# Group 0 of a four-layer sequence kernel in another order, and the modulator product inside the first gate logit

## The reference

```
h1  = gelu(x3 @ Wn1.T + bn1)                    # line 846, ACT
mod = 0.5 + sigmoid(h1 @ Wn2.T + bn2)           # line 1284 on PE, 855 on ACT
wg  = sigmoid(concat(x3, ema(x3)) @ Wg.T + bg)  # gate logits on PE, scan 1729, tanh 868
tr  = ema(x3 * wg * mod[d], tau[d])  for d in 0, 1   # lines 1737 to 1750 on DVE
out = layernorm((gelu(x3 @ Wsoma.T) * sigmoid(blend(tr) @ Wtemp.T)) @ Wout.T)
```

## Time and profile before

| | us |
|---|---|
| median of 3 runs | 690.83 (690.83 to 690.85) |
| the profiled execution, own time | 691.58 |
| span of the profiled execution | 689.8 |
| PE busy in it | 652.3 |
| DVE busy in it | 551.5 |
| ACT busy in it | 370.0 |
| POOL busy in it | 176.1 |

### The profile page before, as it was taken

How to read it: one execution, slowest core, us unless ns; L and a number is a source line. 1 busy time by engine, 2 the same in 40 slices (tenths; PEclk the granted TensorE clock), 3 DMA queues, 4 the chain that set the end, 5 groups by cost and what they waited for, 6 DMA issues and landing times.

```text
span 689.8 us, 8219 instructions
## 1 busy us (share of the span) xinstructions
PE 652.3 (95%) x2848; PEld 491.8 (71%) x2848; DVE 551.5 (80%) x792; ACT 370.0 (54%) x759; POOL 176.1 (26%) x268
## 2 busy tenths in 40 slices
PE   3989989899899999999999999999999999999996
PEld 1545444477677878787878787888787878787875
DVE  2685877869997998799879987998799749974955
ACT  1143368666476357635764576357635743574244
POOL 5003412211065025411441154114411210121001
PEclk9999999999999999999999999999999999999999
DMA  6988999996048844562456335634463320031001
GB/s 205 329 304 287 269 248 313 335 342 163 0 56 156 152 64 100 119 95 54 101 133 104 60 94 116 96 62 98 111 97 61 50 74 0 1 56 68 1 0 61
DMA packets 51575, 86.83 MB, mean 126 GB/s; under 512 B 8256, under 2 KB 10304, under 8 KB 51406
## 3 DMA queue, kind: packets, MB, share of 16 engines
q0 software_dynamic: 16896, 33.56, 30.5%
q1 hardware_dynamic: 31134, 52.74, 21.3%
q10 hardware_dynamic: 3504, 0.01, 0.3%
HBM read 63.22 MB, written 22.04 MB: 124 GB/s over the span
## 4 chain that ended last, share of the span: by engine, by line
PE 60%; DVE 22%; ACT 7%; issue 6%; DMA 3%; SPq 1%; POOLq 0%; POOL 0%; ACTq 0%; DVEq 0%
PE bank L1177 16%; PE bank L1178 16%; PE bank L1179 16%; DVE tr L1750 5%; PE bank L1074 3%; DVE tr L1741 2%; ACT mod L855 2%; DVE wgb L1737 2%; DMA xts<-in_xT 2%; PE bank L1173 2%; DVE wgb L1729 2%; PE bank L1253 2%; DMA beside_scratch<-xts 1%; DVE tr L1758 1%; ACT wgb L868 1%
## 5 line engine op out<-in xcount | busy, mean ns | idle before, releaser
L1750 DVE TENSOR_TENSOR_SCAN tr<-alpha,carry,tr 128x512 f32<-128x512 f32 x48 | 58.9, 1267 | 0.0
L642 POOL TENSOR_TENSOR rs_a<-ss_a,consts 128x1 f32<-128x1 f32 x32 | 16.0, 499 | 143.3 <-ACT junk_f L822 143.0
L1177 PE MATMUL bank<-th,wg_l 128*128 128x512 f32 x128 | 51.9, 406 | 0.0
L1177 PE MATMUL bank<-xh,wg_l 128*128 128x512 f32 x128 | 51.9, 406 | 0.0
L1178 PE MATMUL bank<-xl,wg_h 128*128 128x512 f32 x128 | 50.5, 394 | 0.0
L1178 PE MATMUL bank<-tl,wg_h 128*128 128x512 f32 x128 | 50.5, 394 | 0.0
L1179 PE MATMUL bank<-xh,wg_h 128*128 128x512 f32 x128 | 50.2, 392 | 0.0
L1179 PE MATMUL bank<-th,wg_h 128*128 128x512 f32 x128 | 50.2, 392 | 0.0
L874 ACT ACTIVATE carry<-tr 128x2 f32<-128x2 f32 x32 | 6.6, 206 | 80.3 <-DVE tr L1750 80.3
L1737 DVE SCALAR_TENSOR_TENSOR wgb<-wgb,soma 128x512 f32<-128x512 f32 x32 | 22.0, 687 | 30.5 <-ACT wgb L868 30.5
L602 POOL TENSOR_TENSOR late_side_f<-x2b 128x510 f32<-128x510 f32 x24 | 28.3, 1177 | 56.8 <-DMA x2b<-x_scratch 26.1
(11 more groups left out here) (290 smaller groups left out, 2011.3 us busy)
## 6 DMA issues: line engine op xcount, KB each, us to landing
x2b<-beside_scratch POOLq DMA_DIRECT2D x12, 1024.0 KB, 9.1
xr<-rows_scratch POOLq DMA_DIRECT2D x10, 1024.0 KB, 10.2
xb<-in_x SPq DMA_DIRECT2D x8, 1024.0 KB, 14.6
result<-xr SPq DMA_DIRECT2D x7, 1024.0 KB, 4.3
beside_scratch<-xts SPq DMA_DIRECT2D x6, 1024.0 KB, 11.2
x2b<-rows_scratch POOLq DMA_DIRECT2D x6, 1024.0 KB, 10.9
x_scratch<-xb SPq DMA_DIRECT2D x5, 1024.0 KB, 13.0
x2b<-x_scratch SPq DMA_DIRECT2D x5, 1024.0 KB, 5.5
```

Source lines behind the costliest of these rows:

```text
L642: po.tensor_tensor(rs[:, c:c + 1], ss[:, c:c + 1], eps, ALU.add).then_inc(chain, 1)
L1177: pe.matmul(acc, wl, xh_, start=start, stop=False)
L1750: ve.tensor_tensor_scan(t[:, d], alpha[:, 1 + d:2 + d].broadcast_to([P, GN]), t[:, d], 0.0 if first else carry[:, k, 1 + d:2 + d], ALU.mul ...
```

## The change

In group 0, and at its border with the head:

- **PE**: the x3 transposes of group 0 come before the last three pooled products (tiles 13, 14, 15) instead of after them.
- **DVE**: `ln_apply(0, c)` are no longer alternated with x1 tiles; x1 of tiles 9 to 12 follow the fourth `ln_apply`; then the zeroed edge, `x3_lo(0)`, `late_by_local(2, 0)`, x1 of tiles 13 to 15, `weight2_low(1)`, and only then `late_stencil(2, 0)`.
- **ACT**: `x3_evict(0)` comes before `late_mix(2, 0)`; `weight_hi(0)` and the GELU follow at once; `late_mix(2, 1)` comes after the GELU; `scale_beside(6)` and `scale_beside(7)` move behind `late_mix(2, 2)` and `late_mix(2, 3)`, into the traces of group 0.
- **SP**: `store_beside(6)` comes after `store_x1(7)` and the load of the temporal weight.

In all eight groups, on PE: the modulator product (line 1284) stands between the two halves of gate logit 0 (after 12 of its 24 matmuls) instead of after all 24.

```diff
--- before.py
+++ after.py
@@ -501,11 +501,11 @@
                             sp.wait_ge(x1_done, NT + 1)
                             sp.dma_start(ws_st, chunks(wsoma)).then_inc(w2_in[0], 16)
                     store_x1(6)
-                    store_beside(6)
                     store_x1(7)
                     sp.wait_ge(x1_out[4], 16)
                     sp.wait_ge(x1_out[5], 16)
                     sp.dma_start(wt_st[:], chunks(wtemp)).then_inc(w2_in[1], 16)
+                    store_beside(6)
                     store_beside(7)
                     sp.wait_ge(x1_out[6], 16)
                     sp.wait_ge(x1_out[7], 16)
@@ -990,17 +990,16 @@
                     scale_beside(4)
                     scale_beside(5)
                     act.wait_ge(x1_out[3], 16)
+                    x3_evict(0)
                     late_mix(2, 0)
-                    x3_evict(0)
-                    late_mix(2, 1)
-                    scale_beside(6)
                     weight_hi(0, ws_h[:], ws_st)
-                    scale_beside(7)
                     for g in range(GROUPS):
                         adapted = g < LAST
                         late = g + 3 < GROUPS
                         n1_gelu(g)
-                        if 0 < g and g + 2 < GROUPS:
+                        if g == 0:
+                            late_mix(2, 1)
+                        elif g + 2 < GROUPS:
                             late_mix(g + 2, GT - 1)
                         mod_tanh(g)
                         keep_ctx(g, 0)
@@ -1008,12 +1007,14 @@
                         mod_affine(g)
                         if g == 0:
                             late_mix(2, 2)
+                            scale_beside(6)
                         keep_traces(g, 0)
                         keep_ctx(g, 1)
                         sigmoid_gate(g, 1)
                         trace_hi(g, 0)
                         if g == 0:
                             late_mix(2, 3)
+                            scale_beside(7)
                         keep_traces(g, 1)
                         keep_ctx(g, 2)
                         sigmoid_gate(g, 2)
@@ -1275,25 +1276,29 @@
                                 pe.wait_ge(o_w, GT * (g - 1) + k - 1)
                             elif k == 2:
                                 pe.wait_ge(x1_done, NT * B)
-                            gate_logits(g, k).then_inc(ctx_mm, 1)
+                            logits_now(g, k)
                             if k == 0:
-                                pe.wait_ge(x3T_hi, KE * g + 3)
-                                pe.wait_ge(n1_act, g + 1)
-                                if g == 0:
-                                    pe.wait_ge(wn2_set, 2)
-                                pe.matmul(bank[MOD][:], wn2_half[:], nar[:], start=True, stop=True)\
-                                  .then_inc(mod_mm, 1)
-
-                    def gate_logits(g, k):
-                        acc = bank[CTX[k]][:]
+                                modulators(g)
+                            logits_before(g, k).then_inc(ctx_mm, 1)
+
+                    def modulators(g):
+                        pe.wait_ge(x3T_hi, KE * g + 3)
+                        pe.wait_ge(n1_act, g + 1)
+                        if g == 0:
+                            pe.wait_ge(wn2_set, 2)
+                        pe.matmul(bank[MOD][:], wn2_half[:], nar[:], start=True, stop=True).then_inc(mod_mm, 1)
+
+                    def logits_now(g, k):
                         xh, xl = x3_pair(g)
+                        for i in ks:
+                            split3(bank[CTX[k]][:], wg_h[:, KE + i, chunk(k)], wg_l[:, KE + i, chunk(k)],
+                                   xh[:, i], xl[:, i], i == 0, False)
+
+                    def logits_before(g, k):
                         bh, bl = before_pair(g)
                         for i in ks:
-                            split3(acc, wg_h[:, KE + i, chunk(k)], wg_l[:, KE + i, chunk(k)], xh[:, i], xl[:, i],
-                                   i == 0, False)
-                        for i in ks:
-                            last = split3(acc, wg_h[:, i, chunk(k)], wg_l[:, i, chunk(k)], bh[:, i], bl[:, i],
-                                          False, i == KE - 1)
+                            last = split3(bank[CTX[k]][:], wg_h[:, i, chunk(k)], wg_l[:, i, chunk(k)],
+                                          bh[:, i], bl[:, i], False, i == KE - 1)
                         return last
 
                     def soma_in(g, k, adapted):
@@ -1428,9 +1433,11 @@
                     pooled(1, 6)
                     pooled(1, 7)
                     first_up()
-                    for c in range(8, NT):
+                    for c in range(8, 13):
                         pooled(1, c)
                     x3_transposes(0)
+                    for c in range(13, NT):
+                        pooled(1, c)
                     for g in range(GROUPS):
                         adapted = g < LAST
                         front(g)
@@ -1846,21 +1853,20 @@
                     x1(1, 7)
                     ln_weigh(0, 2)
                     ln_weigh(0, 3)
+                    ln_apply(0, 0)
                     x1(1, 8)
-                    ln_apply(0, 0)
-                    x1(1, 9)
                     ln_apply(0, 1)
-                    x1(1, 10)
                     ln_apply(0, 2)
-                    x1(1, 11)
                     ln_apply(0, 3)
-                    for c in range(12, NT):
+                    for c in range(9, 13):
                         x1(1, c)
                     zero_edge(0)
+                    x3_lo(0)
                     late_by_local(2, 0)
-                    x3_lo(0)
+                    for c in range(13, NT):
+                        x1(1, c)
+                    weight2_low(1, ws_h[:], ws_l[:], ws_st)
                     late_stencil(2, 0)
-                    weight2_low(1, ws_h[:], ws_l[:], ws_st)
                     late_by_local(2, 1)
                     late_stencil(2, 1)
                     assert n["p"] == S_PARAMS, n["p"]
```

## The result

| | us |
|---|---|
| before, median of 4 runs | 690.83 (690.72 to 690.85) |
| after, median of 4 runs | 685.65 (685.09 to 687.4) |
| ratio | 0.992, 95% interval 0.9904 to 0.9937 |
| the profiled execution after, own time and span | 687.4 and 685.6 |

The account below looks back on a forecast made before the run. PE was taken as the bound from group 1 on, DVE in group 0. Group 0's 3.1 and the steady groups' 2.6 made 5.7 us, taking the median from 690.83 to 685.1, range 683.2 to 688.2.

Parts of the forecast that it names:

- Turning x3: Border of head and group 0, PE: x3 transposes start at 126.9 instead of 129.38; n1 starts at 132.3.
- GELU first: Group 0, ACT: table load near 135.5, modulator product at 137.9 instead of 143.48, tanhs over by 141.9 instead of 147.4.
- The new last arrival: Group 0: late tiles 0 and 1 hold the scan of logit 0 until 143.1, with 0.5 us of POOL stretch.
- The gain of group 0: DVE's chain of group 0 starts 3.1 us earlier, bounds 2.9 to 3.6, and group 0 ends 3.1 earlier.
- group 0 gains more: Rival in group 0: late tiles quicker, no stretch, pooled products at 1.1; 684.2 to 683.4 us; chance 0.14.
- The scalings: Traces of group 0, ACT: each scale_beside of 2.0 us fits idle time of about 3 us and costs nothing.
- The late landing: Rival: store_beside(6) lands at 162 to 166.6, DVE's trace_lo(0, 0) waits; 1.4 to 6.0 us lost; chance 0.13.
- The steady groups: Groups 1 to 7: modulator product inside logit 0 starts DVE's chain 1.5 earlier; together 2.6 us, bounds 0 and 2.8.
- The gaps: Group 0, PE: idle gaps before the down, up and temporal products stay, about 1.3 to 1.7 us.

## Why the prediction was right

I had 685.1 us and the measurement 685.65; against its own trace the forecast of -5.7 stands beside -6.1. The plain runs thus give 0.9 less than the trace; two of the four ran at a mean granted clock of 0.994, which the forecast has no term for. By its steps (times of after less 1.94):

- **Turning x3**: 126.86, predicted 126.9. n1 began at 131.94, predicted 132.3: the pooled products started 1.09 apart and not 1.20, which I had taken as the most.
- **GELU first**: table load at 134.9 (predicted 135.5), the modulator product at 137.5 with no idle before it (137.9), tanhs at 139.2 (139.1). That they would wait for the soma weight's low half I had not seen. ACT stood 1.61 before them, of which this wait is the last 0.5 (the tanhs begin 1.66 after their product and not 1.14). It cost nothing, as the scan came later still.
- **The new last arrival** was named rightly: POOL's tile 1 behind the first stencil. POOL began at 132.25 (predicted 132.6), the edge column was stretched by 0.44 (taken as 0.5, with bounds of 0 and 0.7), and the scan ran at 142.8 (143.1). Moving the stencil proved it: 1.24 more. The gain of group 0 is 3.41 instead of 3.1, inside its bounds of 2.9 to 3.6, and the difference is the spacing of the pooled products, which was one part of the rival "group 0 gains more". (That rival's 684.2 is this spacing and no stretch; its lower end, 683.4, has no sum behind it.)
- **The scalings** fit: 1.17 of idle time is left before the carry copy at 151.34, where 3.07 was the earlier trace rows. They cost nothing where they stand and 2.1 where they stood.
- **The late landing** did not occur. The store of tile 6 was issued at 150.2, as foreseen, and took 4.3 us; I expected 6 to 9, from 1.5 MB still queued, which no run shows. It was needed at 162.22.
- **The steady groups** gave 2.7 for 2.6: the gap of group 3 and the small ones went, and DVE's chain in group 3 starts 1.5 earlier, counted from its GELU. DVE's idle time before the gate product fell by 2.4, where I had named 1.5 as the sign: the scan ahead of it also starts later by the 0.9 that my own sum has.
- **The gaps** before down and up, 1.52 and 1.53, are as predicted; the one before the temporal products (1.19) is as it was the earlier trace rows and under the 1.3 that I gave as the lower end.

What the forecast did not say is that the parts depend on each other, and how little the border with the head is worth. ACT's order alone gave 1.3, the split alone nothing, the two together 5.5 of the 6.1, and DVE's order without the early turning is a loss. The forecast counted group 0 as one sum of 3.1 and named no share for the early turning; 2.9 came without it. Nor did I price a stand of PE by more than its length, which is where my number for the split alone failed.

## What to carry to other kernels

Move a producer ahead first, then the instruction that waits for it: a product placed early in PE's queue is a gain only if its input is already there, and otherwise a stand of the bottleneck. Where PE's gaps all end with one engine, look at that engine's own idle time. Moving the stencil took 1.66 us of idle time off DVE and gained 1.2; moving the temporal weight's low half took none off, so the gap came back at the next thing in its queue, larger by what others then waited for. Before giving DVE work to GpSimd, look at which DVE operations run beside it: two-input ones on SBUF paid back nearly all that was saved (2.1 of 2.2 us).

## What the runs showed of the hardware

- **The clock after a stand.** PE stood 3.87, 3.18 and 4.43 us in three kernels and each time a piece at the lower level followed; after a stand of 2.45 also (granted clock 0.76, 0.50 and 0.88 in the three windows of 2 us from 170 to 176, with the temporal weight's half on POOL). After 3.37 none followed in the profiled execution, and after the stands of 1.2 to 1.7 us before the down, up and temporal products none did in any trace.
- **The same order, with and without.** Ahead of the early turning PE is thinly used. In the kernels with the output weight's half on POOL and with SP as before it was busy for the same 0.62 of the 2 us from 122 to 124; the clock stayed at 1.00 in the one and was 0.50 from 126 to 128 in the other. Of the nine traces with this order three have the piece. In the head the kernel after had one at 88 to 94 in one profile and at 78 to 82 in the other. H lay at 119.8 to 120.7 in the three traces with a head piece at 88 to 94 and at 116.9 to 119.4 in the others. So one program has such a piece in one execution and not, or elsewhere, in the next. That this also spreads the plain runs fits their mean granted clocks, but no trace of them shows it. The Trainium skill (TensorE: Matmul & The Clock Gate, Part 1) says that a gate can halve the clock in the middle of a kernel, and that the number of slow matmuls at a kernel's start varies from run to run. The traces agree with the first (1.00 to 0.50) and show the like of the second inside the kernel.
- **The price.** Matmuls of 512 columns started 0.43 apart instead of 0.23. One piece cost 1.2 to 1.6 us in S1 and some 1.9 in the head of the profiled kernel after, but about 0.1 before group 1's output products, where DVE decides: there the turning came 1.8 and 3.0 later and S2 grew by 1.9 and 3.1.
- **Two SBUF inputs against POOL, both ways.** In after DVE's last `x3_lo` took 1.45 instead of 0.69 beside POOL's operation of 1.04, and POOL's edge column behind it 0.67 instead of 0.23. In the kernel with ACT's order and the split the same column, behind a DVE operation of four times the length, took 2.25:

```profile
137.17 2.25 POOL L604 TENSOR_SCALAR late_side_f<-x2b 128x1 f32<-128x1 f32 x1
```

```profile
136.46 2.88 DVE L1667 TENSOR_TENSOR ws_l<-prob,ws_h 128x2048 fp32r<-128x2048 f32 x1 [0.45 <-ACT ws_h L929]
```
